# Router weights by broadcast loads in place of products with the identity, in the first expert layer of a four-part graph network

## The reference, cut to what matters

```python
v = jnp.clip(x @ v_w + v_b, -3.0, 3.0)
a = (-2.0 + v).astype(jnp.complex64) - 1j
G = bk_green_diag(a)                  # a forward and a backward recurrence over the 625 nodes
feats = jnp.stack([G.real, G.imag], axis=-1)
probs = jax.nn.softmax(x @ gate_w + gate_b, axis=-1)
topv, topi = jax.lax.top_k(probs, 2)
topv = topv / jnp.sum(topv, axis=-1, keepdims=True)
comb = jnp.sum(topv[..., None] * jax.nn.one_hot(topi, E, dtype=x.dtype), axis=2)
h = jax.nn.gelu(jnp.einsum('bnd,edf->bnef', x, w1) + b1)
y = jnp.einsum('bnef,efd->bned', h, w2) + b2
ffn_out = jnp.einsum('bne,bned->bnd', comb, y)
spec_out = jnp.clip(feats, -10.0, 10.0) @ out_w + out_b
return ffn_out + bk_scale * spec_out
```

## Time and profile before

| | |
|---|---|
| time, median of 3 runs (lowest to highest) | 1713.42 us (1709.91 to 1715.22) |
| time of the profiled execution | 1722.29 us |
| its span | 1720.4 us |
| mean granted TensorE clock | 0.910 |
| busy: PE, PEld, DVE, ACT, POOL | 1501.9, 1203.1, 945.8, 526.2, 575.7 us |
| DMA | 244.61 MB, mean 142 GB/s |
| store of xn (page, part 6) | 1920 KB, median 8.7 us to landing |

### The profile page before, as it was taken

The page is one execution under the profiler, slowest core; times in us unless marked ns, Lnnn a source line. Parts: engine busy times, 40 slices in busy tenths (PEclk is TensorE's granted clock), DMA queues, the critical chain, the costliest instruction groups (busy, mean ns, idle before and its releaser), DMA issues.

```text
span 1720.4 us, 23475 instructions
## 1 busy us (share of the span) xinstructions
PE 1501.9 (87%) x8128; PEld 1203.1 (70%) x8128; DVE 945.8 (55%) x2162; ACT 526.2 (31%) x565; POOL 575.7 (33%) x500
## 2 busy tenths in 40 slices
PE   8999947759689979779999999999978979699992
PEld 7888637755466645379999999999856655456661
DVE  6643868852534381245666566665547751346664
ACT  0001033421211000055555555555435540113330
POOL 0000277777666661022222222222157720101102
PEclk9998978769689989779999999999988899899996
DMA  7006500000231101167778777777669860415734
GB/s 191 22 0 6 113 2 1 1 1 1 56 113 30 30 2 5 55 230 280 278 274 277 273 278 276 283 278 279 234 227 315 262 188 1 127 39 153 227 117 164
DMA packets 112316, 244.61 MB, mean 142 GB/s; under 512 B 30069, under 2 KB 51762, under 8 KB 112156
## 3 DMA queue, kind: packets, MB, share of 16 engines
q1 hardware_dynamic: 77292, 137.32, 25.9%
q0 software_dynamic: 22432, 72.27, 15.1%
q10 hardware_dynamic: 12528, 34.22, 5.0%
HBM read 202.93 MB, written 45.29 MB: 144 GB/s over the span
## 4 chain that ended last, share of the span: by engine, by line
PE 72%; DVE 14%; DMA 5%; issue 5%; ACT 3%; POOL 1%; another core or an unknown queue 0%; DVEq 0%; ACTq 0%; SPq 0%; POOLq 0%; PEldq 0%
PE PS L2238 21%; PE PS L1977 7%; PE PS L2200 5%; PE PS L2151 4%; PE PS L2386 4%; DMA xg<-xn_dram,xrow 3%; PE PS L2348 3%; PE PS L2397 3%; PE PS L2333 3%; PE PS L2228 2%; DVE e L1084 2%; PE PS L2110 2%; PE PS L2011 2%; PE PS L2122 2%; PE PS L2369 2%
## 5 line engine op out<-in xcount | busy, mean ns | idle before, releaser
L667 POOL DMA_INDIRECT xg<-xn_dram,xrow x70 | 120.5, 1722 | 450.0 <-DVEq L1272 356.4
L2238 PE MATMUL PS<-whi,xhi 128*128 128x384 f32 x840 | 219.8, 342 | 2.3 <-DVEq L1594 2.3
L2238 PE MATMUL PS<-whi,xlo 128*128 128x384 f32 x840 | 214.3, 336 | 0.0
L2238 PE MATMUL PS<-wlo,xhi 128*128 128x384 f32 x840 | 214.1, 335 | 0.0
L1084 DVE TENSOR_TENSOR wlo<-raw,whi 128x2304 fp32r<-128x2304 f32 x72 | 184.6, 2564 | 49.4 <-ACTq L882 42.5
L880 ACT ACTIVATE whi<-raw 128x2304 fp32r<-128x2304 f32 x72 | 153.7, 2135 | 16.1 <-ACT xhi L890 5.7
L2238 PEld LDWEIGHTS PS<-whi,xlo 128*128 128x128 f32 x840 | 152.2, 188 | 0.0
L2238 PEld LDWEIGHTS PS<-wlo,xhi 128*128 128x128 f32 x840 | 151.9, 188 | 0.0
L2238 PEld LDWEIGHTS PS<-whi,xhi 128*128 128x128 f32 x840 | 148.3, 189 | 2.6 <-DVEq L1594 2.6
L1084 DVE TENSOR_TENSOR xlo<-PS,xhi 128x768 fp32r<-128x768 f32 x70 | 67.0, 958 | 140.0 <-ACTq L891 135.0
L1977 PE MATMUL PS<-hot_dr,hot_s 125*125 125x512 bf16 (+9 forms) x880 | 134.5, 301 | 5.9 <-DVE hot_dr L1141 5.9
(11 more groups left out here) (374 smaller groups left out, 2544.3 us busy)
## 6 DMA issues: line engine op xcount, KB each, us to landing
raw<-in_L_gnn_W_rel SPq DMA_DIRECT2D x72, 1152.0 KB, 7.7
z_dram<-xn ACTq DMA_DIRECT2D x70, 384.0 KB, 7.3
raw<-in_L_ffn_w SPq DMA_DIRECT2D x12, 576.0 KB, 6.0
y_dram<-yb ACTq DMA_DIRECT2D x17, 384.0 KB, 3.9
pre<-in_L_ffn_w SPq DMA_DIRECT2D x9, 576.0 KB, 5.3
gw<-in_L_gnn_W SPq DMA_DIRECT2D x2, 2304.0 KB, 27.2
fw<-in_L_ffn_w SPq DMA_DIRECT2D x8, 576.0 KB
fw<-in_L_ffn_w SPq DMA_DIRECT2D x1, 4608.0 KB, 16.0
```

The source lines that it names most:

```text
L667: pool.indirect_dma_start(xg[b][j][:, :], None, xn_dram, bass.IndirectOffsetOnAxis(ap=xrow[:, b, j:j + 1], axis=0)).then_inc(x_gathered[b] ...
L2238: mm = pe.matmul(slot(q)[:, s * BANK:s * BANK + HALF], a[:, k, :], wt[:, k, s * HALF:(s + 1) * HALF], start=(k == 0 and part == 0), stop=( ...
```

## The change

1. The router weights reach VectorE by another way. ScalarE copies combT as before and signals comb_turned; SyncE stores it to comb_dram (8 x 625), waits, and loads for each pair of experts three tiles combw (128 x 625) by four loads that repeat one row of DRAM over 64 or 128 partitions. VectorE multiplies hT by these tiles. `widen`, `weights_row` and `weights_chunk` are gone; chunks 2 to 11 follow each other.
2. The load of the second layer's weights (fw2) and SyncE's wait for evw_ready move behind these loads.
3. `outer` waits for inner_done chunk by chunk at tile 0 rather than for all twelve ahead.
4. combT and feats share one tile of 35 rows (0 to 7, 32 to 34, zeros between), b2r and specw another; one product of 35 rows stands for the two. VectorE clears both tiles at the end of the layer before.
5. VectorE normalises each tile right after its residual add. xn is stored in five pieces, and turned by tile (`TURN4`); the gathers wait for all five.
6. raw no longer lies over hT but over fw1: its first load waits for ScalarE's last gelu, and ScalarE makes the high part of relation 0 ahead of the root of tile 4. The later tiles (wroot, rbrow, gate, hh) are placed anew.

```diff
-    ("turn3", [0, 3, 2, 0]), ("route1", [0, 0, 1, 2]), ("inner1", [6, 6, 6, 6]),
+    ("turn3", [0, 3, 2, 0]), ("route1", [0, 0, 1, 2]), ("inner1", [6, 6, 0, 0]),
...
-    ("turn4", [2, 2, 1, 1]), ("relations", [REL + EXTRA, REL, REL + EXTRA, REL]),
+    ("turn4", [0, 2, 2, 1]), ("relations", [REL + EXTRA, REL, REL + EXTRA, REL]),
...
+TURN4 = [(1, 0), (2, 0), (3, 0), (1, 1), (2, 1)]
...
-            combw = [sb(f"combw{b}", [P, T, 2 * F], f32, g) for b in range(2)]
+            combw = [[sb(f"combw{b}_{c}", [128, N], f32, g) for c in range(3)] for b in range(2)]
...
+        SPEC = 32
+        combT, feats, small_left = hT[0:NE, FK, :], hT[SPEC:SPEC + 3, FK, :], hT[0:SPEC + 3, FK, :]
+        b2r, specw, small_right = fw2[0:NE, FK, :], fw2[SPEC:SPEC + 3, FK, :], fw2[0:SPEC + 3, FK, :]
...
         # SyncE
             load_pair(fw1[1], w1v, 1, ld_f1[1])
-            sp.wait_ge(evw_ready, 1)
             sp.wait_ge(layer_done, 1)
...
-            sp.dma_start(fw2[:, 0:FK, :], ...).then_inc(ld_f2, 16)
...
             through_dram(1, v_dram.rearrange("(t p) -> p t", p=P), v_col[:, :], vch[:, :], ...)
+            sp.wait_ge(comb_turned, 1)
+            sp.dma_start(comb_dram, combT).then_inc(comb_stored, 16)
+            sp.wait_ge(comb_stored, 16)
+
+            def load_comb(i):
+                if i >= 2:
+                    sp.wait_ge(inner_done, 3 * (i - 1))
+                for c, first, end, e in ((0, 0, 128, 2 * i), (1, 0, 64, 2 * i), (1, 64, 128, 2 * i + 1), (2, 0, 128, 2 * i + 1)):
+                    sp.dma_start(combw[i % 2][c][first:end, :], comb_dram[e, :].partition_broadcast(end - first)).then_inc(combw_loaded[i % 2], 16)
+
+            load_comb(0)
+            load_comb(1)
             load_next_pair(2)
+            load_comb(2)
             load_next_pair(3)
+            load_comb(3)
+            sp.wait_ge(evw_ready, 1)
+            sp.dma_start(fw2[:, 0:FK, :], ...).then_inc(ld_f2, 16)
             through_dram(2, mat_dram, ...)
...
-            sp.wait_ge(layer_done, 2)
+            sp.wait_ge(act_done, FK + 1)
...
             load_raw(0, True)
-            sp.wait_ge(xn_ready, 4 * T)
-            sp.dma_start(xn_dram.rearrange("(t p) d -> p t d", p=128), xn_all[:, :, :]).then_inc(xn_stored, 16)
+            for t in range(T):
+                sp.wait_ge(xn_ready, 3 * T + t + 1)
+                sp.dma_start(xn_dram[t * 128:(t + 1) * 128, :], xn_all[:, t, :]).then_inc(xn_stored, 16)
...
         # GpSimd
-            pool.wait_ge(xn_stored, 16)
+            pool.wait_ge(xn_stored, 16 * T)
...
         # ScalarE
+            act.sem_inc(comb_turned, 1)
+            for c in range(2, FK):
                 gelus(c, c % 2, c // 2)
...
+            for t in range(T):
+                if t == T - 1:
+                    act.wait_ge(specw_ready, 1)
+                    act.wait_ge(spec_in, 64)
+                    w_high(0, 0, 0, 1)
+                root(var_ready, STD_BEFORE[3] + t + 1, rstd[:, t:t + 1], t5[:, 0, t:t + 1])
...
         # VectorE
+            do(dve.memset(small_left, 0.0))
+            do(dve.memset(small_right, 0.0))
             dve.sem_inc(layer_done, 1)
...
-            widen(0, 0)
-            widen(1, 1)
             for c in range(FK):
+                i = c // 3
                 dve.wait_ge(act_done, c + 2)
-                dve.wait_ge(full[2 + c % 2], BEFORE["inner1"][2 + c % 2] + c // 2 + 1)
-                do(tt(hT[:, c, :], hT[:, c, :], slot(2 + c % 2)[:, 0:N], ALU.mult))
-                free_slot(2 + c % 2)
+                dve.wait_ge(combw_loaded[i % 2], 64 * (i // 2 + 1))
+                do(tt(hT[:, c, :], hT[:, c, :], combw[i % 2][c % 3][:, :], ALU.mult))
                 dve.sem_inc(inner_done, 1)
-                if c % 3 == 2 and c // 3 + 2 < NE // 2:
-                    widen(c // 3 + 2, c // 3 % 2)
...
+                if t == T - 1:
+                    dve.sem_inc(layer_done, 1)
+                norm_tile(3, x_res, t)
...
         # TensorE
-            inner_chunk(2)
             pe.wait_ge(comb_ready, 1)
...
-            for c in range(3, FK):
-                weights_chunk(c - 3)
+            for c in range(2, FK):
                 inner_chunk(c)
-            for c in range(FK - 3, FK):
-                weights_chunk(c)
...
+                            if stage == "outer1" and t == 0:
+                                pe.wait_ge(inner_done, c + 1)
...
-                    pe.matmul(o, combT[:, t * P:(t + 1) * P], b2r[:, s * HALF:(s + 1) * HALF], start=False, stop=False)
-                    mm = pe.matmul(o, feats[:, t * P:(t + 1) * P], specw[:, s * HALF:(s + 1) * HALF],
+                    mm = pe.matmul(o, small_left[:, t * P:(t + 1) * P], small_right[:, s * HALF:(s + 1) * HALF],
                                    start=False, stop=True)
...
-            pe.wait_ge(inner_done, FK)
...
-            turn("turn4", xn, lambda: pe.wait_ge(xn_ready, 4 * T))
+            for t in range(T):
+                q, k = TURN4[t]
+                take("turn4", q, k)
+                pe.wait_ge(xn_ready, 3 * T + t + 1)
+                for c in range(K):
+                    mm = pe.transpose(slot(q)[:, c * 128:c * 128 + P], xn[:, t, c * 128:(c + 1) * 128], ident[0:P, 0:P])
+                mm.then_inc(full[q], 1)
```

More of the change, by code:

```diff
@@ L84 @@
 TURN_W2 = [("turn", 0)] + [job for t in range(1, T) for job in (("turn", t), ("product", t - 1))] + [("product", T - 1)]
-XT_TURNED = [0, K, K + T] + [2 * T + n * K for n in range(1, 5)]
+XT_TURNED = [0, K, K + T, K + 2 * T] + [3 * T + n * K for n in range(1, 4)]
 BEFORE, _n = {}, [0, 0, 0, 0]
@@ L330, in build @@
             v_col = sb("v_col", [P, T], f32, g)
[L332 to L335, removed]
+        SPEC = 32
+        combT, feats, small_left = hT[0:NE, FK, :], hT[SPEC:SPEC + 3, FK, :], hT[0:SPEC + 3, FK, :]
+        b2r, specw, small_right = fw2[0:NE, FK, :], fw2[SPEC:SPEC + 3, FK, :], fw2[0:SPEC + 3, FK, :]
+        bkrow = fw2[SPEC:SPEC + 3, FK + 1, :]
         g = ExitStack()
         with g:
+            LOW = 14 * N + 2
+            wlo = [sb("wlo0", [128, K, D], f32r, g)]
+            xg = [[sb(f"xg{b}_{j}", [128, D], f32, g) for j in range(RT)] for b in range(2)]
+            sb("above_xg", [128, LOW - K * D - 2 * RT * D], f32, g)
+            raw = sb("raw", [128, K, D], f32, g)
             whi = [sb(f"whi{b}", [128, K, D], f32r, g) for b in range(2)]
-            wlo = [sb(f"wlo{b}", [128, K, D], f32r, g) for b in range(2)]
-            xg = [[sb(f"xg{b}_{j}", [128, D], f32, g) for j in range(RT)] for b in range(2)]
+            wlo += [sb("wlo1", [128, K, D], f32r, g)]
             xhi = [[sb(f"xhi{b}_{j}", [128, K, 128], f32r, g) for j in range(RT)] for b in range(2)]
@@ L350, in build @@
             pre = sb("pre", [128, SHARED + OWN13 + 2 * OWN2], f32, late)
+            tail = sb("tail", [128, LOW - SHARED - OWN13 - 2 * OWN2], f32, late)
+            rbrow = tail[0:1, 0:D]
+            wroot = sb("wroot", [128, K, D], f32, late)
             s13 = pre[:, 0:SHARED].rearrange("p (k f) -> p k f", k=K)
@@ L724, in _ @@
             pool.sem_inc(earlier_ready, 1)
-            pool.wait_ge(xn_stored, 32)
+            pool.wait_ge(xn_stored, 16 * T + 16)
             for n in range(NE * RT + 1):
@@ L1572, in _ @@
                 pass
-            def add_result(stage):
-                for t in range(T):
-                    q = t % 4
-                    dve.wait_ge(full[q], BEFORE[stage][q] + t // 4 + 1)
-                    xr = x_res[:, t, :].rearrange("p (b c) -> p b c", b=2)
-                    do(tt(xr, slot(q).rearrange("p (b c) -> p b c", c=BANK)[0:P, :, 0:HALF], xr, ALU.add))
-                    free_slot(q)
-            add_result("outer1")
-            dve.sem_inc(layer_done, 1)
-            norm(3, x_res)
+            for t in range(T):
+                q = t % 4
+                dve.wait_ge(full[q], BEFORE["outer1"][q] + t // 4 + 1)
+                xr = x_res[:, t, :].rearrange("p (b c) -> p b c", b=2)
+                do(tt(xr, slot(q).rearrange("p (b c) -> p b c", c=BANK)[0:P, :, 0:HALF], xr, ALU.add))
+                free_slot(q)
+                if t == T - 1:
+                    dve.sem_inc(layer_done, 1)
+                norm_tile(3, x_res, t)
             KH = K // 2
@@ L2153, in inner @@
                 return mm
-            def weights_row(q, b, c):
-                for t in range(T):
-                    for o, p0, n in piece(0, t * P, P):
-                        mm = pe.matmul(slot(q)[:, p0:p0 + n], combw[b][:, t, c * 128:(c + 1) * 128],
-                                       ident[0:P, o:o + n], start=True, stop=True)
-                mm.then_inc(full[q], 1)
             def inner_chunk(c):
```

40 lines of the change are left out of this document (15 added, 25 removed).

## The result

The changed kernel took 1668.64 us (median of 4 runs, 1663.34 to 1672.14), the kernel before 1711.66 on the same chip (4 runs, 1704.11 to 1715.22). The ratio is 0.9752 with an interval of 0.9709 to 0.9795: 2.5% faster. Measured once more, with six runs on another chip, it was 1661.65 against 1708.12, 0.9731 (0.9693 to 0.9770). The 50 us of the first two traces had let expect 0.9705 there, a gain partly given back 0.975 or more; it lies between. Forecast were 1661.0 us and a range of 1652 to 1678. The profiled execution has a span of 1666.3 us, a time of 1668.15 and a mean granted clock of 0.918; before, these were 1720.4, 1722.3 and 0.910.

What follows compares the result with a forecast made beforehand. TensorE, 72% of the chain, was taken as the bound, so the gain is how much earlier the first relation product starts. The terms summed to 52.4 us, giving 1661.0 us from the median 1713.4, range 1652 to 1678.

Steps and rivals of the forecast that it cites:

- first products and waiting: Expert layer's first products up to the first outer product: without router-weight rows and the long wait, 26.0 us less.
- outer products, tiles 0 to 3: Outer products of four tiles run at the full-clock price after a shorter wait: 2.6 us less.
- small products, tiles 0 to 3: Four records a tile in place of eight, all at the full clock: 10.2 us less.
- small products, tile 4: Merged small products of the last tile fall from 2.8 to 1.3 us: 1.5 us less.
- outer products, tile 4: The last tile's outer products take the full-clock 15.6 us in place of 17.59: 2.0 us less.
- normalisation of one tile on the path: Before the relations, only tile 4's add and normalisation, 3.7 us, stay on the path: 7.7 us less.
- store of one tile: The last xn store is 384 KB, taken as 3.9 us in place of 8.29: 4.4 us less.
- gathers beside raw: Relation 1's raw loads now start with the gathers before the first relation product: 2.0 us more, bounds 0 to 4.
- Weights off TensorE: Router weights reach VectorE by broadcast loads, their cost all covered; up to the first outer product 26.0 us less.
- The rival of late loads and VectorE: In the first half, fw2 or multiplies come late and stall 2 to 8 us: gain about 46, 1667; chance 0.10.
- The rival of slow broadcasts: Broadcast loads hold back fw2 and become the bound; break-even 22.8 us a set, 1734 at 28; chance 0.04.
- The rival of a gain taken back at the handover: Before the relations, DMA state holds the start, so normalisation and store give nothing: 12.1 us less gain, 1673; chance 0.10.

Runs made afterwards that it cites:

- handover alone: The kernel before with only normalisation, store and transposes of xn done tile by tile: 1700.13 us, ratio 0.9957.
- weights alone: The kernel before with only router weights by broadcast loads, fw2 loaded later and chunk-wise waits of the outer products: 1689.14 us, ratio 0.9842.
- points 2 and 3 undone: The changed kernel with fw2 loaded early again and one wait for all twelve multiplies ahead of the outer products: 1661.76 us, ratio 0.9722.
- between: The changed kernel with small products of tiles 0 and 1 after the third outer tile, 2 and 3 after the fourth: 1664.51 us, ratio 0.9700.
- the held load: The changed kernel with the loads of relation 1's matrix held until relation 1's gathered tile has landed: 1657.67 us, ratio 0.9710.
- Both undoings: The changed kernel with one normalisation of five tiles and one store of xn, timed twice: 1671.54 us, ratio 0.9761, and 1665.74 us, ratio 0.9744.

## Why the prediction was right, and where its sizes were off

By its terms, forecast and read from the trace after:

| term | forecast | measured |
|---|---|---|
| first products and waiting | -26.0 | -26.2 |
| outer products, tiles 0 to 3 | -2.6 | -2.7 |
| small products, tiles 0 to 3 | -10.2 | -8.4 |
| small products, tile 4 | -1.5 | -1.3 |
| outer products, tile 4 | -2.0 | -0.2 |
| normalisation of one tile on the path | -7.7 | -7.5 |
| store of one tile | -4.4 | -6.0 |
| gathers beside raw | +2.0 | +1.7 |
| sum | -52.4 | -50.5 |

Of the rest of the 54.1 us between the two spans, 3.5 are a first expert product that came earlier (494.53 against 498.01), ahead of all that was changed. Two errors of size partly cancel in the sum: 3.6 us too much hoped for from the clock, 1.6 too little from the store.

**Weights off TensorE: right.** The stretch is the transposes, ten chunks at 6.50 and a wait of 0.99 (forecast 1.1). Times of this part are to be read with the 3.5 us by which it all began earlier. The first multiply came at 533.48, so 0.5 us later after the first expert product than the forecast's 536.5 has it. The window from 531 to 536 has 273 GB/s, but a weight load issued at 531.23 is in it; set 2, alone from 541 to 544 us, moved at 214 GB/s, close to the 218 taken. fw2 was issued at 554.44 (557 forecast) and the window from 571 to 576 us has only 42 GB/s left, so it landed near 571, at the early end of the 575 to 579 forecast. The mat_dram round trip came without delay, 571.76 to 573.14. The rival of late loads and VectorE failed with that: multiplies 9 to 11 began at 579.08, 584.70 and 590.30, about one us ahead of the forecast even with the 3.5 taken off, and each of the twelve took 0.81 us as with its input from PSUM. The Trainium skill, "SBUF — State Buffer", section "SBUF: two separate sides", says that a VectorE operation with two SBUF inputs and a GpSimd operation that reads SBUF take a shared port in turns, each for its whole length. GpSimd's indirect stores were under way all along, and no lengthening is seen here; whether such a store counts as such an operation the runs don't show. The rival of slow broadcasts is out for the same 533.48: its break-even was 22.8 us a set.

**Small products and tile 4's outer products: two terms mis-sized, with one cause.** The forecast put the new stretch of 5.2 us right at the 5.4 after which the clock had fallen, and chose that it wouldn't. It fell after 3.6. The 3.6 us too much in the two terms are that choice, a little more than the 3 that it had allowed for; the stated bound for tile 4 (+1) held. Two steps of it failed. The moment was read from one execution and taken as fixed: with the small products as before it was 5.6, 5.0 and 3.7 us in three executions (before, handover alone, weights alone), with the merged ones 3.3 to 5.2 in seven. And a fall at the very end wouldn't have been free, as the 17.3 us with points 2 and 3 undone show. That the loss is the clock's is shown by *between*: same products, same number, clock at 1.00, 3.0 us less.

**Handover: right, store mis-sized.** The prediction's 678.5 for tile 4's end is 677.7 by its own terms, which changes nothing. From the last add to the end of xn are 4.0 us (3.7 forecast, 11.5 before), and the store took 2.30 rather than 3.9. The row taken for it was the median of stores issued among others; it is 3.1 in the profile after. The estimate of 2.9 by the Trainium skill ("DMA: Bandwidth & Descriptors", section "Anatomy of one DMA — SWDGE (gpsimd) path"), whose figures are for DMAs issued by GpSimd while this one is SyncE's, was nearer, and still too long. The store alone doesn't tell the gain, though: with one store of 6.66 the way from its landing to the product was 1.6 us shorter.

**Gathers: right in size and, by the held load, in cause.** +1.7 against +2.0. Holding raw took 2.0 us off the same stretch between executions whose stores took 5.1 and 5.5 us, and 3.5 off that of the profile after, whose store was short; both lie within the bounds of 0 to 4. The rival's expectation, that the 14.4 us are the gathers' own, is out.

**The rival of a gain taken back at the handover** had normalisation and store give nothing. Both undoings cost 10 us in the trace, so it is out as a mechanism. Its number, 1673, is near the first median of 1668.6, and that stays the open part: the trace has 50.5 us for the change, the medians 43.0 and 46.5. The lower bounds of the two ratios, 50 and 52 us, just reach it. Two things on record bear on it. Stretches that the change leaves alone differ by up to 10 us from one execution to the next, so medians of a few runs move by some us with them: a second profile of the changed kernel has the same inner and outer (95.2 and 108.5) in a span 9.9 us shorter. And the profile before is a long one in the changed stretch too: with the handover alone, inner, which that change leaves as it was, took 118.7 us in place of 121.4, with the router's products 3.0 us shorter. What part of the 4 to 7 us is that was not settled.

## What to carry to other kernels

Values that an engine spreads over partitions by products with the identity can come from DRAM instead where the loads have idle queues and many microseconds of lead: here the stretch of first products fell from 121.4 us to 95.2. Behind such a removal read the next two or three waits in the chain and count the queue of each; a median from the page's list of DMAs is that of its neighbours' traffic, so take the windows around the place. And where the forecast stands on a clock that fell near the edge of a new stretch, read the moment in several executions first, and price the other side too; a version with the stretch cut into small pieces settles more than a choice of side.

## What the runs showed of the chip

- TensorE's granted clock fell from 1.00 to 0.50 (2.4 to 1.2 GHz) while it was continuously busy with products of few rows: 3.7 to 5.6 us into them in three executions with eight records a tile, 3.3 to 5.2 in seven with four, 3.2 when each was made twice. Groups of 2.77 us were followed by the fall in one kernel (0.2 and 0.6 us behind their end) and not in another with the same order; groups of 1.48 us never in the one execution seen.
- The 60 records of the router's products of 9 columns took 10.8 to 10.9 us in eight executions and 7.8 to 8.0 in six, in kernels with the same code there. The difference is the granted clock: it fell 2.0 to 2.2 us into them in the eight, 5.1 to 5.4 in the six; what decides when it falls no run here shows. Both are in the chains above: 10.87 at 503.39 after, 7.81 at 503.77 with raw held. The windows of these two, after first:

```profile
503.39:505.30 1.91, 1.91 (x19) 1.91 (x19) 0.00 (x0) 1.69 (x3) 1.60 (x2) 1.00 0.07 2
505.30:514.26 8.96, 8.96 (x45) 8.96 (x44) 0.00 (x0) 1.84 (x2) 5.08 (x7) 0.50 0.06 1
```

```profile
503.77:509.00 5.23, 5.23 (x50) 5.23 (x49) 0.00 (x0) 3.53 (x4) 4.01 (x5) 1.00 0.07 2
509.00:511.58 2.58, 2.58 (x14) 2.58 (x14) 0.00 (x0) 0.00 (x0) 2.11 (x2) 0.50 0.10 2
```

- Loads that repeat one 2.5 KB row over 128 or 64 partitions moved at 214 GB/s where they were alone (541 to 544 us, DMA share 0.70), at about half the rate of the plain load of fw2 (419 GB/s from 561 to 566 us, share 1.03). This set was 960 KB, and SyncE took 2.1 us to issue its four loads.

```profile
541.00:544.00 3.00, 3.00 (x12) 1.56 (x12) 2.18 (x12) 0.70 (x1) 0.87 (x3) 1.00 0.70 214
561.00:566.00 5.00, 5.00 (x21) 2.85 (x20) 1.88 (x10) 0.78 (x1) 2.69 (x4) 1.00 1.03 419
```

- A 384 KB store took 2.30 us with still queues and 5.1 to 5.5 us behind a load of small records. That load was issued between 657.7 and 671.1 us in executions with the same work before it, so part of the scatter between runs probably lies there; where the raw loads weren't held, the way behind the longer store was 1.4 us shorter, so less than 2 of the 3 us reach the total.
